# A selective-scan recurrence: some drives scaled on ScalarE in turned layout, other shared states, z projected at the start of the unit

## The chip, the cores and the metric

One core of one Trainium2 chip runs the whole kernel. The metric is device time in microseconds of one launch. The engines named below are TensorE (PE, its weight loads PEld), VectorE (DVE), ScalarE (ACT), GpSimd (POOL) and SyncE (SP), which here issues the DMA transfers of the recurrence. PSUM is 8 banks of 128 x 512 f32; four tiles of two banks each are all of it in this stage.

## The reference, cut to what matters

The input is (4, 64, 32, 32). A bidirectional Mamba layer with a group norm comes first, then attention, then a spectral filter with mixed experts. The change touches the first only. For each of 4 images, in both directions:

```python
xz = x @ W_in                               # 64 -> 256, halves xp and z
xc = silu(xprev * conv_w[:, 0] + xp * conv_w[:, 1] + conv_b)
dt_r, Bc, Cc = split(xc @ W_x)              # 8, 16, 16
dt = softplus(dt_r @ W_dt + b_dt)           # 128 channels
h = exp(dt * A[s]) * h + (dt * xc) * B[s]   # for each of 16 states s, over 1024 tokens
y = sum over s of h[s] * C[s] + D * xc
y = y * silu(z);  out = y @ W_out           # then group norm, silu, residual
```

## The kernel before, in words

A **unit** is one image in one direction: 8 units, u = 0 to 7, the image's forward one (i = 0) and then its backward one (i = 1). Tiles are [128 channels, 1024 tokens] f32. Unit 0 and 1 are written out, units 2 to 5 are a loop over images, units 6 and 7 are written out again, and unit 7 (the final one) also does the start of the attention of the first image. Everything runs in program order on each engine; semaphores tie the engines together.

Each unit runs 16 states. For a state, in the ordinary (own) form: ACT makes the decay exp(dt * a[s]) in one of three SBUF tiles (`decay_of`, L731); DVE multiplies dt*x (in PSUM, `ps_x`) by the row B[s], which a DMA has spread over 128 partitions (`b_wide`), into `ps_d` (`drive_step`, L871), and scans (`scan_step`, L876, the scan itself L888) into one of four `hidden` tiles; POOL multiplies this by the spread row C[s] into one of four `prod` tiles (L455); PE adds the product to `ps_y` with an identity matmul (`sum_states`, L547), three states late (`Y_LAG`).

Five states of a unit, 2, 3, 6, 9 and 15, are **shared**: POOL makes the drive, from an SBUF copy of dt*x (`share`, L441, the multiply L445), and ACT writes the decay to PSUM (`shared_decay_of`, L737): for 3, 6 and 9 (`WIDE_SHARED`) into `ps_w`, for 2 and 15 into `ps_d`. Unit 7 shares only state 6.

`ps_w` also carries the preparation of the next unit v = u + 1, between those decays: the projection of z (`gate_in`, L493, after state 15 of the unit before has been summed, at s == 2) and ACT's copy of it (`take_z`, L668), the projection of xp (`conv_in`, L498) and `silu_input` (L674), `low_rank` (L504) and `take_low`, and `dt_in` (L511), which may start when the scan of the last wide shared state, 9, has read its decay. `softplus_exp` and `softplus_ln` (L699 to L720) are six ACT operations in a row; PE sums their parts in `ps_w` (L518 to L539), ACT takes dt (L722), DVE makes dt*x (`dt_x`, L857) ahead of the scan of state 15, and ACT copies it to SBUF (`keep_dtx`, L726). In ACT's order the decay of state s + 2 stands at s, ahead of what else is done at s; so the decays of states 13 and 14 stand behind softplus, which is at s == 10.

After the scan of state 1 DVE gates the sum of the unit before (`gate_of`, L864, the multiply L869): it waits until PE has added all its 16 products. After it PE starts `ps_y` anew with D*xc (`skip_in`, L541, a diagonal matmul), and in forward units first does the output product (`out_product`, L555), which ACT must have taken (`norm_take`, L686) before `skip_in`.

SP issues the loads in its own order: for each state a B row, which waits until the drive that used its buffer is done (four buffers), and the C row of the state before, which waits for a product (L372 to L394).

## Time and profile before

| | us |
|---|---|
| median of 3 runs | 949.39 (944.57 to 951.92) |
| the profiled execution | 949.59 |
| its span | 947.8 |
| mean granted TensorE clock | 0.955 |
| units 0 to 7 with what leads to them | about 0 to 488 |

The page gives the busy time of each engine over the span; the windows give it by stretch. The timelines of the engines list instructions in order of time, runs of like ones merged, with the idle time before them and what ended it. A matmul with f32 operands of 512 columns appears as two records, so one `sum_states` is four. Throughout, T is the time from the start of the scan of state 15 of the unit before.

### The profile page before, as it was taken

Reading aid. Unit: us, or ns where it says so; the run is one execution under the profiler, and the core shown is the slowest. Engines: PE = TensorE matmul, PEld = TensorE weight load, DVE = VectorE, ACT = ScalarE, POOL = GpSimd, SP = SyncE. Lnnn points to the kernel's source line nnn. Section 1 sums busy time; section 2 is a strip of 40 time slices with the busy share of each in tenths; the row PEclk is TensorE's granted clock in tenths of the full one; section 3 lists DMA queues with packets and bytes.
Section 4 is the critical chain, followed back from the end, with each engine's and each line's share of the span. In section 5 each row is a group of like instructions: output and inputs, shape, how many; then the busy total and the mean of one; then the engine's idle time right before and its main releaser. Section 6 shows DMA issues by size and latency. Waiting matters only on the chain. (4 is left out here: it accounts for less than half of the span.)

```text
span 947.8 us, 10164 instructions
## 1 busy us (share of the span) xinstructions
PE 830.0 (88%) x2974; PEld 488.3 (52%) x2974; DVE 712.0 (75%) x767; ACT 508.8 (54%) x702; POOL 549.8 (58%) x373
## 2 busy tenths in 40 slices
PE   5579897979899898986587899989999999999996
PEld 1224332433334333332144554558888888888885
DVE  1999999999999999999965455646665665565664
ACT  3645666556566666643315446446555554555553
POOL 4678989999998998975736955312212221212210
PEclk9799999999999999987987999999999999999999
DMA  7969897888979898796509800001442443243342
GB/s 180 329 201 331 311 339 277 334 309 307 311 271 379 301 321 304 285 333 222 201 0 139 155 0 1 1 1 53 125 133 92 130 125 98 90 133 99 123 116 61
DMA packets 75348, 178.22 MB, mean 188 GB/s; under 512 B 24514, under 2 KB 25044, under 8 KB 75300
## 3 DMA queue, kind: packets, MB, share of 16 engines
q1 hardware_dynamic: 75316, 177.85, 57.9%
q8 instruction: 13, 0.21, 0.1%
q14 instruction: 19, 0.16, 0.1%
HBM read 175.57 MB, written 2.26 MB: 188 GB/s over the span
## 5 line engine op out<-in xcount | busy, mean ns | idle before, releaser
L455 POOL TENSOR_TENSOR prod<-hidden,c_wide 128x1024 f32<-128x1024 f32 x128 | 300.3, 2358 | 63.5 <-DVE hidden L888 58.1
L551 PE MATMUL ps_y<-prod,ident 128*128 128x512 f32 x512 | 242.8, 618 | 30.8 <-POOL prod L455 30.6
L888 DVE TENSOR_TENSOR_SCAN hidden<-decay,ps_d 128x1024 f32<-128x1024 f32 x92 | 209.9, 2282 | 8.3
L1919 PE MATMUL ps_conv<-hankel,u_high 128*128 128x512 f32 (+1 forms) x768 | 215.3, 361 | 0.0
L551 PEld LDWEIGHTS ps_y<-prod,ident 128*128 128x128 f32 x512 | 98.2, 197 | 171.3 <-issue 117.4
L1919 PEld LDWEIGHTS ps_conv<-hankel,u_high 128*128 128x128 f32 x768 | 138.6, 189 | 25.5 <-DVE u_t L1786 0.2
L1919 PE MATMUL ps_conv<-hankel,u_low 128*128 128x512 f32 (+1 forms) x384 | 138.1, 360 | 0.0
L2033 DVE TENSOR_TENSOR stack<-ps_conv,stack 64x512 fp32r<-64x512 f32 x128 | 88.3, 690 | 62.1 <-ACT stack L2000 59.6
L1751 POOL CAST block_mix<-even 128x256 fp32r (+1 forms) x32 | 12.7, 398 | 208.5 <-PE sums L1792 208.5
L2033 DVE TENSOR_TENSOR qk<-ps_conv,qk 64x512 fp32r<-64x512 f32 x128 | 88.3, 689 | 50.2 <-ACT qk L2000 47.5
L874 DVE TENSOR_TENSOR ps_d<-ps_x,b_wide 128x1024 f32<-128x1024 f32 x92 | 113.4, 1232 | 4.6
L2000 ACT ACTIVATE stack<-ps_conv 64x512 fp32r<-64x512 f32 x128 | 76.0, 594 | 74.3 <-PE ps_conv L1919 72.4
L2000 ACT ACTIVATE qk<-ps_conv 64x512 fp32r<-64x512 f32 x128 | 76.0, 593 | 63.2 <-PE ps_conv L1919 61.2
L445 POOL TENSOR_TENSOR drive<-dtx,b_wide 128x1024 f32<-128x1024 f32 x36 | 84.9, 2359 | 7.5 <-ACT dtx L729 7.1
L1919 PEld LDWEIGHTS ps_conv<-hankel,u_low 128*128 128x128 f32 x384 | 72.8, 190 | 13.8
L734 ACT ACTIVATE decay<-dt_b,a_neg_b 128x1024 f32<-128x1024 f32 x48 | 53.2, 1140 | 35.9 <-DVE hidden L888 35.6
L888 DVE TENSOR_TENSOR_SCAN hidden<-ps_w,drive 128x1024 f32<-128x1024 f32 x22 | 50.1, 2279 | 0.0
L734 ACT ACTIVATE decay<-dt_f,a_neg_f 128x1024 f32<-128x1024 f32 x44 | 48.2, 1137 | 2.0 <-DVE dt_f L852 0.9
L1472 DVE TENSOR_REDUCE max_parts<-sums 128x1 f32<-128x512 f32 (+1 forms) x48 | 27.5, 598 | 26.6 <-PE sums L1147 17.0
L1060 POOL TENSOR_TENSOR small<-small,minus_half 128x8 f32<-128x8 f32 x4 | 6.6, 1646 | 56.4 <-DVE small L1442 56.4
L1340 ACT ACTIVATE probs<-ps_t 128x512 f32<-128x512 f32 (+1 forms) x48 | 24.8, 521 | 22.8 <-PE ps_o L1192 22.4
L1792 PE MATMUL sums<-stack,block_mix 128*128 128x512 f32 (+1 forms) x160 | 32.5, 349 | 2.1 <-DVE stack L2033 2.1
(283 smaller groups left out, 1154.3 us busy)
## 6 DMA issues: line engine op xcount, KB each, us to landing
b_wide<-bc_rows SPq DMA_DIRECT2D x128, 512.0 KB, 5.6
c_wide<-bc_rows SPq DMA_DIRECT2D x128, 512.0 KB, 5.5
hankel<-filters SPq DMA_DIRECT2D x32, 1026.0 KB, 5.3
plus<-in_M_phi_plus SPq DMA_DIRECT2D x2, 1024.0 KB, 12.9
minus<-in_M_phi_minus SPq DMA_DIRECT2D x2, 1024.0 KB, 18.1
x_pair<-in_x SPq DMA_DIRECT2D x2, 768.0 KB, 8.3
bc_rows<-mixed_and_low SPq DMA_DIRECT2D x8, 128.0 KB, 4.9
out<-plus SPq DMA_DIRECT2D x4, 256.0 KB, 5.0
```

Of the source, the lines that this page charges most:

```text
L445: nc.gpsimd.tensor_tensor(drive[DRIVE_OF[s]][:, :], dtx[:, :], b_wide[s % BC_DEEP][:, :], ALU.mult).then_inc(share_ready, 1)
L455: nc.gpsimd.tensor_tensor(prod[k % PAIR][:, :], hidden[k % DEEP][:, :], c_wide[s % BC_DEEP][:, :], ALU.mult).then_inc(prod_ready, 1)
L551: mm = nc.tensor.matmul(out, ident[:, :], halves(prod[k % PAIR])[h], start=False, stop=(k % N == N - 1))
L734: nc.scalar.activation(decay[decay_slot(s, last)][:, :], dt[i][:, :], ACT.Exp, scale=a_neg[i][:, s:s + 1]).then_inc(decay_ready, 1)
L874: nc.vector.tensor_tensor(ps_d[:, :], ps_x[:, :], b_wide[s % BC_DEEP][:, :], ALU.mult).then_inc(drive_ready, 1)
L888: nc.vector.tensor_tensor_scan(hidden[k % DEEP][:, order], left[:, order], right[:, order], 0.0, ALU.mult, ALU.add).then_inc(hidden_ready, 1)
L1340: nc.scalar.activation(probs[n % 2][:, 0:hi - lo], ps_t[n % 2][:, 0:hi - lo], ACT.Exp).then_inc(probs_ready, 1)
L1472: nc.vector.tensor_reduce(max_parts[:, i, at // H:at // H + 1], ps_s[c % 2][:, 0:n], AX.X, ALU.max, negate=True).then_inc(part_ready, 1)
L1792: return nc.tensor.matmul(dst, w_block, data, start=first, stop=True, skip_group_check=True)
L1919: mm = nc.tensor.matmul(out, pairs[q][wp][:, 2 * delta + source, :], rows, start=(delta == 0 and term == 0), stop=(delta == 2 * half + 1 a ...
L2000: nc.scalar.activation(stacks[slot][0:C, source, b, :, half * 2 * HEAD:(half + 1) * 2 * HEAD], ps_conv[source][lanes(b), half, :, :], ACT. ...
L2033: nc.vector.tensor_tensor(low, ps_conv[source][lanes(b), half, :, :], high.bitcast(F32), ALU.subtract).then_inc(conv_low, 1)
```

## The change

- The shared states are 3, 7, 10, 15, of which 3, 7 and 10 are wide (in unit 7: state 6).
- States 2, 4, 8, 11 (in unit 7: 2, 7) are **turned**: PE transposes dt*x and the rows of B once per unit (`turn_dtx`, 8 + 8 transposes of 128 tokens, into `ps_w`), ACT copies them to SBUF (`take_turned`, three copies). With tokens on partitions, B[s] is a column, and ACT scales 8 tiles of 128 x 128 with it (`scale_drive`, 8 instructions); PE transposes the 8 back into `ps_d` (`turn_drive`), and DVE scans from there. DVE has no `drive_step` for these and SP no B row.
- `gate_in` stands at s == 0 and waits for the three copies; `take_z`, the decays and the new work have other places in ACT's order.
- `dt_in` stands at s == 11 and waits for the scan of state 10; the exponential's sum stands at s == 13 and the logarithm's at s == 14.
- D*xc is written to `ps_y` by ACT (`skip_in`, with a scale per channel) instead of by PE, and relu(dt) stays in `ps_w` instead of being added by PE. There is one `xc` tile instead of two.
- Three `b_wide` buffers instead of four, used in turn by the 12 states that still need a row.

```diff
-POOL_STATES = (2, 3, 6, 9, 15)
-WIDE_SHARED = POOL_STATES[1:4]
+POOL_STATES = (3, 7, 10, 15)
+TURNED_STATES = (2, 4, 8, 11)
+WIDE_SHARED = POOL_STATES[0:3]
+B_DEEP = 3
...
+        LAST_SHARE = (6,)
+        LAST_TURNED = (2, 7)
...
                 def spread_b(u, i, s):
-                    if u or s >= BC_DEEP:
-                        drive_done(*divmod(u * N + s - BC_DEEP, N))
-                    spread(b_wide[s % BC_DEEP], i * 2 * N + s, b_in[s % BC_DEEP])
+                    slot = b_slot(i, s, u // 2 == B - 1)
+                    if slot in held:
+                        drive_done(*held[slot])
+                    held[slot] = u, s
+                    spread(b_wide[slot], i * 2 * N + s, b_in[slot])
...
                 def gate_in(u, i, b):
-                    pe.wait_ge(dtx_ready, u)
+                    pe.wait_ge(dtx_t_ready, 3 * u)
                     project(i, b, w_gate[i], z_ready)
...
+                def turn_dtx(u):
+                    def turn(half):
+                        for t in range(half * SPANS, (half + 1) * SPANS):
+                            mm = nc.tensor.transpose(ps_w[:, t * 128:(t + 1) * 128], dtx[:, t * 128:(t + 1) * 128], ident[:, :])
+                        mm.then_inc(dtx_turned, 1)
+                    pe.wait_ge(dtx_kept, u + 1)
+                    turn(1)
+                    for t in range(TILES):
+                        mm = nc.tensor.transpose(ps_w[:, t * C:(t + 1) * C], dt_low[BC_ROW:, t * 128:(t + 1) * 128],
+                                                 ident[BC_ROW:, BC_ROW:])
+                    mm.then_inc(dtx_turned, 1)
+                    pe.wait_ge(dtx_t_ready, 3 * u + 2)
+                    turn(0)
+                def turn_drive(u, s, last=False):
+                    scanned(u, s - (2 if s - 1 in wide(last) else 1))
+                    for half in range(2):
+                        pe.wait_ge(drive_t_ready, 2 * turned_before(u, s, last) + half + 1)
+                        for t in range(half * SPANS, (half + 1) * SPANS):
+                            mm = nc.tensor.transpose(ps_d[:, t * 128:(t + 1) * 128], drive_t[turned_slot(s, last)][:, t, :], ident[:, :])
+                    mm.then_inc(drive_turned, 1)
...
                             if s == Y_LAG:
+                                turn_drive(u, s - 1, not ahead)
                                 if i == 0 and not first:
                                     out_product(b - 1)
+                                if s + 1 in turned(not ahead):
+                                    turn_drive(u, s + 1, not ahead)
+                                if i == 0 and not first:
                                     conv_in(v, j, bv)
-                                    pe.wait_ge(g.mixed_ready, b)
-                                skip_in(u, i)
-                            if s == 13 and ahead:
+                            if s == 14 and ahead:
                                 add_logarithm(v, j)
                             if not (first and k < Y_LAG):
-                                sum_states(n - Y_LAG, (k - Y_LAG) % (2 * N))
+                                sum_states(n - Y_LAG, (k - Y_LAG) % (2 * N), u if s == Y_LAG else None)
+                            if s > Y_LAG and s + 1 in turned(not ahead):
+                                turn_drive(u, s + 1, not ahead)
                             if ahead:
-                                if s == 2:
+                                if s == 0:
...
                                     gate_in(v, j, bv)
...
-                                if s == (7 if i == 1 or first else 5):
+                                if s == (8 if i == 1 or first else 7):
                                     scanned(u, WIDE_SHARED[1])
                                     low_rank(v, j)
-                                if s == 10:
+                                if s == 11:
                                     scanned(u, WIDE_SHARED[2])
                                     dt_in(v, j)
-                                if s == 11:
-                                    add_rectified(v)
-                                if s == 12:
+                                if s == 13:
                                     add_exponential(v)
+                                if s == N - 1:
+                                    turn_dtx(v)
...
+                def skip_in(u, i, taken=0):
+                    at_least(act, gated_ready, u)
+                    at_least(act, g.mixed_ready, taken)
+                    nc.scalar.activation(ps_y[:, :], xc[:, :], ACT.Copy, scale=cols[i][:, 1:2]).then_inc(skip_ready, 1)
+                def take_turned(u):
+                    def take(n, half):
+                        act.wait_ge(dtx_turned, 3 * u + n + 1)
+                        nc.scalar.activation(dtx_t[:, half * SPANS:(half + 1) * SPANS, :].rearrange("p t d -> p (t d)"),
+                                             ps_w[:, half * H:(half + 1) * H], ACT.Copy).then_inc(dtx_t_ready, 1)
+                    at_least(act, drive_turned, TURNED * u)
+                    take(0, 1)
...
+                    take(2, 0)
+                def scale_drive(u, s, last=False):
+                    act.wait_ge(dtx_t_ready, 3 * u + 3)
+                    at_least(act, drive_turned, turned_before(u, s, last) - 1)
+                    for t in range(TILES):
+                        part = nc.scalar.activation(drive_t[turned_slot(s, last)][:, t, :], dtx_t[:, t, :], ACT.Copy, scale=b_t[:, t, s:s + 1])
+                        if t % SPANS == SPANS - 1:
+                            part.then_inc(drive_t_ready, 1)
...
+                            if s == 0:
+                                take_z(v, j, first=first and i == 0)
+                                shared_decay_of(u, i, WIDE_SHARED[0], z_taken, v)
+                                decay_of(u, i, 2)
+                            if s == 1:
+                                scale_drive(u, 4)
+                                decay_of(u, i, 4)
                             if s == 2:
...
+                                decay_of(u, i, 5)
...
+                                if first or i == 1:
+                                    skip_in(u, i)
                                 silu_gate(v, j)
                                 if not first:
                                     if i == 0:
                                         norm_take(b - 1)
+                                        skip_in(u, i, taken=b)
                                     else:
                                         norm_silu(nc, act, g, b - 1)
                                 silu_input(v, j)
...
                             if s == 4:
+                                decay_of(u, i, 6)
                                 shared_decay_of(u, i, WIDE_SHARED[1], xc_ready, v + 1)
+                            if s == 5:
+                                scale_drive(u, 8)
+                            if s == 6:
+                                decay_of(u, i, 8)
+                                decay_of(u, i, 9)
...
+                                scale_drive(u, 11)
                             if s == 7:
                                 take_low(v, j)
                                 shared_decay_of(u, i, WIDE_SHARED[2], dt_low_ready, v + 1)
+                            if s in (9, 10, 11, 12):
+                                decay_of(u, i, s + AHEAD)
...
                             if s == N - 1:
...
                                 keep_dtx(v)
                                 decay_of(v, j, 1, last and i == 0)
+                                take_turned(v)
+                                if TURNED_STATES[0] in turned(last and i == 0):
+                                    scale_drive(v, TURNED_STATES[0], last and i == 0)
```

## Rows read from the trace of the kernel before

**Rows 1.** Windows: busy time by stretch, granted clock, DMA share
```profile
core 0: us, PE busy (x) PEld busy (x) DVE busy (x) ACT busy (x) POOL busy (x), PEclk, DMA share, GB/s
...
230.00:300.00 70.00, 64.74 (x143) 26.13 (x143) 67.67 (x41) 44.34 (x44) 64.39 (x29) 0.98 0.90 322
```

**Rows 2.** Line L729 (dtx copied), all eight, and the second alone
```profile
L729 ACT ACTIVATE dtx<-ps_x x8: 1024/1024/1030, 28.0 to 409.7; 128x1024 f32<-128x1024 f32 x8
...
L729 ACT ACTIVATE dtx<-ps_x x1: 1030/1030/1030, 86.1 to 86.1; 128x1024 f32<-128x1024 f32 x1
```

**Rows 3.** Timeline of DVE: start, us, instruction, in unit 4
```profile
246.53 1.21 DVE L862 TENSOR_TENSOR ps_x<-ps_w,xc_f 128x1024 f32<-128x1024 f32 x1
247.80 2.29 DVE L888 TENSOR_TENSOR_SCAN hidden<-ps_d,drive 128x1024 f32<-128x1024 f32 x1
...
257.44 1.20 DVE L869 TENSOR_TENSOR gated_b<-ps_y,gate_b 128x1024 f32<-128x1024 f32 x1
...
271.56 2.28 DVE L888 TENSOR_TENSOR_SCAN hidden<-ps_w,drive 128x1024 f32<-128x1024 f32 x1
273.76 2.26 DVE L888 TENSOR_TENSOR_SCAN hidden<-decay,ps_d 128x1024 f32<-128x1024 f32 x1
276.15 1.23 DVE L874 TENSOR_TENSOR ps_d<-ps_x,b_wide 128x1024 f32<-128x1024 f32 x1
...
279.81 1.23 DVE L874 TENSOR_TENSOR ps_d<-ps_x,b_wide 128x1024 f32<-128x1024 f32 x1
280.95 2.28 DVE L888 TENSOR_TENSOR_SCAN hidden<-ps_w,drive 128x1024 f32<-128x1024 f32 x1
```

**Rows 4.** Timeline of PE: sums, the wait for the gate, dt_in
```profile
242.52 8.75 PE L551 MATMUL ps_y<-prod,ident 128*128 128x512 f32 x20
...
258.69 1.97 PE L560 MATMUL ps_y<-gated_f,packed_inner_f 128*64 128x512 f32 x2 [2.41 <-DVE gated_b L869]
...
284.44 1.98 PE L514 MATMUL ps_w<-mixed_and_low,w_dt_b 9*128 9x512 f32 x4
```

**Rows 5.** Timeline of POOL in unit 4
```profile
270.20 6.98 POOL L455 TENSOR_TENSOR prod<-hidden,c_wide 128x1024 f32<-128x1024 f32 x3 [0.90 <-PE ps_y L551]
277.13 2.37 POOL L445 TENSOR_TENSOR drive<-dtx,b_wide 128x1024 f32<-128x1024 f32 x1
279.45 9.29 POOL L455 TENSOR_TENSOR prod<-hidden,c_wide 128x1024 f32<-128x1024 f32 x4
```

**Rows 6.** Timeline of PE: eight transposes of a later stage
```profile
643.46 1.06 PE L1772 MATMUL ps_conv<-ident,u_all 128*128 128x128 f32 x8 [1.14 <-PEq L1044]
```

**Rows 7.** Timeline of ACT in a later stage: eight scaled tiles
```profile
577.69 2.01 ACT L1302 ACTIVATE u_all<-cen,small 128x64 f32<-128x64 f32 x8
```

**Rows 8.** Timeline of ACT, end of unit 3 and in unit 4
```profile
234.69 1.06 ACT L713 ACTIVATE late<-soft 128x1024 f32<-128x1024 f32 x1
...
237.69 2.17 ACT L734 ACTIVATE decay<-dt_b,a_neg_b 128x1024 f32<-128x1024 f32 x2
...
247.85 1.02 ACT L729 ACTIVATE dtx<-ps_x 128x1024 f32<-128x1024 f32 x1
...
286.46 1.03 ACT L704 ACTIVATE soft<-ps_w 128x1024 f32<-128x1024 f32 x1 [4.99 <-PE ps_w L514]
...
289.37 1.06 ACT L713 ACTIVATE late<-soft 128x1024 f32<-128x1024 f32 x1
```

**Rows 9.** Windows of 6 us: the granted clock is the third number from the end
```profile
96.00:102.00 6.00, 4.92 (x8) 2.01 (x8) 5.84 (x4) 5.51 (x5) 6.00 (x3) 0.72 0.76 273
...
366.00:372.00 6.00, 5.22 (x8) 1.37 (x8) 5.84 (x4) 5.21 (x5) 6.00 (x3) 0.72 0.75 263
...
420.00:426.00 6.00, 5.28 (x7) 2.24 (x8) 5.70 (x5) 2.44 (x4) 3.68 (x2) 0.51 0.82 291
```

**Rows 10.** Timelines of DVE and PE in the first unit
```profile
36.63 2.29 DVE L888 TENSOR_TENSOR_SCAN hidden<-ps_d,drive 128x1024 f32<-128x1024 f32 x1 [1.19 <-ACT ps_d L740]
...
26.82 3.50 PE L486 MATMUL ps_w<-x_pair,packed_in_b 128*128 128x512 f32 x4 [4.15 <-DVE ps_x L854]
```

More of the change, by code:

```diff
@@ L297, in mamba_stage, with wide, turned, decayed_before @@
         AHEAD = 2
-        LAST_SHARE = POOL_STATES[2:3]
+        LAST_SHARE = (6,)
+        LAST_TURNED = (2, 7)
         def shared(last):
             return LAST_SHARE if last else POOL_STATES
+        def wide(last):
+            return LAST_SHARE if last else WIDE_SHARED
+        def turned(last):
+            return LAST_TURNED if last else TURNED_STATES
         def driven_before(u, s, last=False):
+            return (N - SHARE - TURNED) * u + s - sum(p < s for p in shared(last) + turned(last))
+        def decayed_before(u, s, last=False):
             return (N - SHARE) * u + s - sum(p < s for p in shared(last))
@@ L307, in shared_before, with turned_before, spread_order, b_slot @@
             return SHARE * u + sum(p < s for p in shared(last))
+        def turned_before(u, s, last=False):
+            return TURNED * u + sum(p < s for p in turned(last))
+        def spread_order(last):
+            return [(i, s) for i in range(2) for s in range(N) if s not in turned(last and i == 1)]
+        UNIT_LOADS = N - TURNED
+        def b_slot(i, s, last):
+            return spread_order(last).index((i, s)) % B_DEEP
+        def b_loads(b, i, s, last):
+            return 16 * (2 * UNIT_LOADS // B_DEEP * b + spread_order(last).index((i, s)) // B_DEEP + 1)
+        def turned_slot(s, last):
+            return turned(last).index(s) % 2
         def own_states(last):
@@ L383, in unit @@
                     for s in range(N):
-                        spread_b(u, i, s)
+                        if s not in turned(u == 2 * B - 1):
+                            spread_b(u, i, s)
                         if u or s:
@@ L475, in _ @@
                 pool.wait_ge(x_in, X_LOADS)
-                share(0, POOL_STATES[0])
                 batch(0, first=True)
@@ L553, in sum_states @@
+                def sum_states(n, k, seeded=None):
+                    pe.wait_ge(prod_ready, n + 1)
+                    if seeded is not None:
+                        pe.wait_ge(skip_ready, seeded + 1)
+                    for h, out in enumerate(halves(ps_y)):
+                        mm = nc.tensor.matmul(out, ident[:, :], halves(prod[k % PAIR])[h], start=False, stop=True,
+                                              skip_group_check=True)
                     mm.then_inc(prod_summed, 1)
@@ L735, in decay_of, with shared_decay_of @@
                                          scale=a_neg[i][:, s:s + 1]).then_inc(decay_ready, 1)
-                def shared_decay_of(u, i, s, taken, count):
+                def shared_decay_of(u, i, s, taken, count, final=False):
                     act.wait_ge(taken, count)
-                    nc.scalar.activation((ps_w if s in WIDE_SHARED else ps_d)[:, :], dt[i][:, :], ACT.Exp,
+                    nc.scalar.activation((ps_w if s in wide(final) else ps_d)[:, :], dt[i][:, :], ACT.Exp,
                                          scale=a_neg[i][:, s:s + 1]).then_inc(share_decay, 1)
@@ L882, in scan_step @@
                         dve.wait_ge(share_ready, shared_before(u, s, final) + 1)
-                        left, right = (ps_w if s in WIDE_SHARED else ps_d), drive[DRIVE_OF[s]]
+                        left, right = (ps_w if s in wide(final) else ps_d), drive[DRIVE_OF[s]]
                     else:
-                        dve.wait_ge(decay_ready, driven_before(u, s, final) + 1)
-                        dve.wait_ge(drive_ready, driven_before(u, s, final) + 1)
+                        dve.wait_ge(decay_ready, decayed_before(u, s, final) + 1)
+                        if s in turned(final):
+                            dve.wait_ge(drive_turned, turned_before(u, s, final) + 1)
+                        else:
+                            dve.wait_ge(drive_ready, driven_before(u, s, final) + 1)
                         left, right = decay[decay_slot(s, final)], ps_d
@@ L930, in batch @@
                                 dve.wait_ge(dtx_kept, 1)
-                            if s in shared(final) and s in WIDE_SHARED:
-                                drive_step(u, s + 1, final)
-                            elif s not in shared(final) and not (s - 1 in shared(final) and s - 1 in WIDE_SHARED):
-                                drive_step(u, s, final)
+                            if s not in shared(final) + turned(final):
+                                drive_step(b, i, s, last)
                             scan_step(u, i, s, final)
```

114 lines of the change are left out of this document (55 added, 59 removed).

## The prediction

> **What bounds the kernel now.** I read the windows by stretch first, to see which engine is full in the recurrence; then the times of the dt*x copies, which mark the units; then the timelines of DVE, ACT, PE and POOL through one unit; then the clock by windows of 6 us. In [rows 1] DVE is busy 67.67 of 70 us, POOL 64.39, PE 64.74 at a granted clock of 0.98 (2.4 GHz), ACT 44.34: DVE sets the pace, with POOL and PE close behind. The copies of dt*x lie at 28.0, 86.1 and 409.7, eight in all [rows 2]: the first unit takes 58.1 us, and the next six (409.7 - 86.1)/6 = 53.93 us each.
>
> DVE's unit can be rebuilt from [rows 3]. An own state, drive and dependent scan, recurs after 279.81 - 276.15 = 3.66 us. A scan that needs no drive costs 273.76 - 271.56 = 2.20. dt_x costs 247.80 - 246.53 = 1.27 and the gate the same. Eleven own and five shared states give 11 x 3.66 + 5 x 2.20 + 2.5 = 53.8, and the norm's few steps 0.3 on average: the 53.93 is DVE with no gap. PE's sum costs 8.75/5, less the modelled tail, 1.72 us; POOL's multiply (9.29 - 2.37)/3 = 2.31 [rows 4, 5].
>
> **The change, part by part.**
>
> *DVE.* Three drives a unit go (11 to 8), each 3.66 - 2.20 = 1.46. The pure work becomes 8 x 3.66 + 8 x 2.20 + 2.5 + 0.3 = 49.7 us, 4.2 less. A scan that reads what PE turned costs the same as one that reads a drive in PSUM, I assume; no row differs.
>
> *PE.* Eight transposes of this shape and type took 1.06 us [rows 6]. A unit has 48 (8 of dt*x, 8 of B, 32 of drives): 6.4 us. It loses the D*xc product and the relu part, 2 x 1.72 = 3.4. It was about 26 blocks of 1.72 = 44.7 in 53.9, and becomes 47.7: no bound by itself. The Trainium skill ("TensorE: Matmul & The Clock Gate", Part 4: PE-mode transpose) gives about 275 ns for a 128 x 128 transpose inside a kernel: 48 of them would be an estimated 13.2 us in place of 6.4. A record here does last some 0.27 us, but they overlap and eight end after 1.06, so the row decides.
>
> *POOL.* 20 multiplies instead of 21, 46.2 us, and one norm or residual step; not the bound in total.
>
> *ACT.* Per turned state 8 scaled tiles. The nearest row is eight of 128 x 64 in 2.01 us [rows 7]; at 128 columns I take 2.35. The lower end is 2.01, the upper one eight with the extra half of the columns unhidden, about 2.8. Four states are 9.4 us, the three copies 1.6 (halves of the 1.02 copy [rows 8]), skip_in 1.1: from 44.34/70 x 53.9 = 34 us to 46. Below DVE's 49.7, but in strict order, so places matter.
>
> *DMA.* 28 row loads a unit instead of 32, at a share of 0.90 [rows 1]. Following the buffers, the row of state 15 waits for the drive of 12 and lands about a microsecond before POOL wants it. I cost it at 0; if it is late, POOL's share of 15 is late by as much.
>
> **Where the gain goes: the start of the unit.** T = 0 is the start of scan 15. dt*x is in SBUF at 1.05 [rows 8]. ACT makes decay 1 until 2.15; PE turns half of dt*x and then B until 2.7; ACT copies both until 3.1; PE turns the other half until 3.75, ACT copies it by 4.4 and scales state 2 by 6.8. All of that round trip lies ahead of PE's sum of state 13, because turn_dtx stands before it in PE's order. So: sum 13 to 5.5, the z projection to 7.3, sum 14 to 9.0, sum 15 to 10.8. The gate waits for sum 15. DVE reaches it at 257.44 - 247.80 = 9.64 today [rows 3]. **Stall 1.2 us**, and behind the gate stand all later scans. The transposes of state 2 (10.8 to 11.8) hide behind the gate.
>
> **The softplus chain.** dt_in writes `ps_w`, so it waits for the last wide shared scan, which was 9 and is now 10. From the start of dt_in to ACT's first step is 286.46 - 284.44 = 2.02 [rows 4, 8]; from there to the fourth operation 289.37 - 286.46 = 2.91; from the fourth to the end of the decay behind the chain, 237.69 + 1.13 - 234.69 = 4.13. Together 9.1 us until decay 13 is there. Between the end of scan 10 and the start of scan 13 DVE has 2.20 + 3.66 + 1.34 = 7.2 of work. **Stall at least 1.9 us in every unit**; before, there was one more drive-and-scan between, 11 us, and the chain just fitted. Moreover dt_in stands behind the sum of state 8, which waits for POOL's product 8, which now comes behind the share of state 10. Following POOL at 2.31 a step: in backward units product 8 is done at 35.5, after a PE backlog dt_in starts at 37.5, decay 13 is there at 46.6, and the next unit's T = 0 is 7.2 later (scan 13, state 14, dt_x): **53.8**. In forward units ACT does the gate's silu and norm_take ahead of skip_in, so the sum of state 0 ends at 21.4, POOL's product 4 starts there (today after a like wait, at 270.20, T + 22.4 [rows 5]), share 10 ends at 35.3, product 8 at 37.6, dt_in starts at 39.4, decay 13 at 48.5: **55.6**. Six units: 3 x 53.8 + 3 x 55.6 = 328.2 against 323.6: **+4.6**.
>
> **First and last unit.** In the first, the round trip and scale 2 take ACT and PE to 36.5, and the z projection is at half clock (3.50 [rows 10] instead of the 1.98 of such four records [rows 4], so I count the transposes double): scan 2 waits for decay 2 until 40.2 instead of 36.63 [rows 10], +3.6; three drives fewer behind it, -4.4; softplus +2.9: **+2.1**. The last unit has no z projection, so sum 15 is in time; it drops two drives, **-2.9**; ACT waits for DVE there and takes the new work in its gaps.
>
> **The clock.** In five of these six units PE's clock fell right after its 2.41 us wait for the gate [rows 4]: the first and last are at 0.72 over 6 us [rows 9], so 6 x 0.28 = 1.7 us lost, half of that stretch at 1.2 GHz. In the last unit, transposes and a 3 us wait were followed by 0.51 [rows 9]. In the new order the thin stretch (wait for dt*x, transposes, round trip) stands right ahead of the four blocks that lead to the gate, so a dip there is on the path: 1.7 us a unit, and nothing absorbs it, as ACT's order shifts with it. I take it in three units of six, **+5.1**; bounds 0 and 10.
>
> Sum: 4.6 + 2.1 - 2.9 + 5.1 = +8.9, on the profiled execution's 949.6: 958.5. That execution and the median of the runs (949.4) agree, so the forecast is 958.5.
>
> **The rivals.**
>
> *A. Only the unavoidable stalls.* If product 8 is never late and no dip is on the path, a unit is 49.7 + 1.2 + 1.9 = 52.8: 6 x -1.1 = -6.8, first unit +1.1, last -2.9: -8.6, 941. For it: POOL is caught up at the end of each unit today, and the gate and chain numbers are tight. Against: the backlog is visible today in PE's run of five sums up to dt_in.
>
> *B. The gain arrives.* If the round trip and the chain are covered, 6 x -4.2, first -0.8, last -2.9: -29, 921. It needs dt_in's chain to be 2 us shorter than the rows; nothing in them says so. The place to see it is decay 13.
>
> *C. Slower by one mechanism, the clock.* A dip in every unit ahead of the gate, twice as long (all four blocks at 3.4 instead of 1.7): 6 x 6.9 = 41 over the 3.8 without dips: 994; with a normal dip in every unit, 10 + 3.8: 963. It decides above 0.9 us a unit. The final unit's row speaks for it; no row shows a whole unit start. The Trainium skill ("TensorE: Matmul & The Clock Gate", Part 4: PE-mode transpose) says that the full clock does not engage for transposes; by that it would be the 994.
>
> *D. ACT's order.* If eight scaled tiles cost 2.8, decays 7 and 10 and the drives of 8 and 11 each come 0.5 to 1.5 late: 1.5 a unit more, 968.
>
> **How the numbers follow.** Forecast (53.8 and 55.6, some dips; 953 to 963): 0.42. A: 0.20. B and what lies between it and A: 0.12. C in its long form and D: 0.26. The range takes A in and D, and leaves out B and C's long form: 940 to 971; the forecast's own is 953 to 963. About 1% (9.5 us) is what a measurement of this kernel can tell from no change. Faster (below 939.9) is B and a part of A: 0.19. Slower (above 958.9) is half of the forecast, C and D: 0.44. The same: 0.37.
>
> **What would show it.** Right: the copies of dt*x 54 to 56 us apart; DVE idle 1 to 3 us before L869's gate, ended by PE's sum, and 2 to 3.6 us before the scan of state 13, ended by ACT's decay; POOL and PE idle more. Transposes of eight in about 1.1 us, eight scaled tiles in 2.0 to 2.8. Wrong: copies closer than 52 us (B); DVE waiting for `ps_d` transposes or for shared decays (D); a mean clock in the recurrence well under 0.9 (C); waits on the B rows. The forecast fails most easily if PE reaches sum 15 before DVE reaches the gate.

## The result and the profile after

The changed kernel takes 980.2 us (977.5 to 983.4), the kernel before 948.7 beside it: 1.033 times as long, with a 95% interval of 1.030 to 1.036. That is slower, as the likeliest sign of the forecast had it, and 9 us outside the range of 940 to 971. The span of the profiled execution went from 947.8 to 975.7 us.

The copies of dt*x mark the units, as in [rows 2]. The line of all eight, and those that begin units 1 to 3 (each from its own stretch), from the changed kernel:

```profile
L792 ACT ACTIVATE dtx<-ps_x x8: 1002/1024/1025, 25.9 to 440.7; 128x1024 f32<-128x1024 f32 x8
...
L792 ACT ACTIVATE dtx<-ps_x x1: 1025/1025/1025, 86.5 to 86.5; 128x1024 f32<-128x1024 f32 x1
...
L792 ACT ACTIVATE dtx<-ps_x x1: 1024/1024/1024, 144.3 to 144.3; 128x1024 f32<-128x1024 f32 x1
L792 ACT ACTIVATE dtx<-ps_x x1: 1024/1024/1024, 204.9 to 204.9; 128x1024 f32<-128x1024 f32 x1
```

The first unit takes 60.6 us (58.1 before). The six after it take (440.7 - 86.5)/6 = 59.0 each, against 53.9: 30.6 us in all. From there to the end of the span is 535.0 us against 538.1. The first copy comes 2.1 us earlier. So +2.5 - 2.1 + 30.6 - 3.1 = +27.9, the whole difference, and it lies in units 1 to 6. (The 2.1 us belong to the start of the program and are not the change's: in the kernels below this copy comes at 25.5 to 28.3.)

The windows over these six units, of the changed kernel and then of the one before (columns as in [rows 1]):

```profile
86.50:440.70 354.20, 314.48 (x864) 145.20 (x864) 292.37 (x171) 271.40 (x412) 285.60 (x126) 0.92 0.72 252
```
```profile
86.10:409.70 323.60, 289.16 (x627) 116.20 (x626) 313.10 (x189) 200.75 (x194) 298.46 (x132) 0.97 0.87 313
```

DVE has 21 us less work and yet the stretch is 31 us longer; the clock is 0.92 instead of 0.97. In the kernel before, DVE's waits in this stretch are too short to be listed. These are its waits now (line waited for, us in total, times, longest):

```profile
DVE hidden L1001 <- ACT decay L820: 29.1, 9, 6.2
DVE gated_f L978 <- PE ps_y L605: 9.4, 3, 3.7
DVE gated_b L978 <- PE ps_y L605: 6.9, 3, 3.6
DVE hidden L1001 <- POOL drive L484: 5.8, 5, 1.9
DVE hidden L1001 <- PE ps_d L596: 2.9, 6, 0.6
DVE hidden L1001 <- issue: 0.5, 1, 0.5
```

They sum to 54.6 us. The removed work was worth 6 x 4.2 = 25 by the rebuilding of the prediction; that leaves a loss of about 30, as the copies have it. What is open here is why the waits are that long, and whether each is a place of its own or one delay seen several times.

In the timeline, a forward unit (4, T = 262.6): DVE and then PE of the changed kernel.

```profile
272.96 1.23 DVE L978 TENSOR_TENSOR gated_b<-ps_y,gate_b 128x1024 f32<-128x1024 f32 x1 [0.78 <-PE ps_y L605]
...
299.56 2.29 DVE L1001 TENSOR_TENSOR_SCAN hidden<-ps_w,drive 128x1024 f32<-128x1024 f32 x1 [1.95 <-POOL drive L484]
...
312.90 2.29 DVE L1001 TENSOR_TENSOR_SCAN hidden<-decay,ps_d 128x1024 f32<-128x1024 f32 x1 [3.45 <-ACT decay L820]
```
```profile
263.51 0.66 PE L578 MATMUL ps_w<-ident,dtx 128*128 128x128 f32 x4 [0.89 <-ACT dtx L792]
264.09 0.71 PE L584 MATMUL ps_w<-ident,mixed_and_low 64*128 64x64 f32 x8
265.20 0.66 PE L578 MATMUL ps_w<-ident,dtx 128*128 128x128 f32 x4 [0.39 <-ACT b_t L804]
265.70 1.98 PE L605 MATMUL ps_y<-prod,ident 128*128 128x512 f32 x4
267.52 1.88 PE L524 MATMUL ps_w<-x_pair,packed_in_b 128*128 x4
269.24 3.60 PE L605 MATMUL ps_y<-prod,ident 128*128 128x512 f32 x8
...
303.69 1.98 PE L552 MATMUL ps_w<-mixed_and_low,w_dt_b 9*128 9x512 f32 x4
```

This is the path that the prediction wrote down: round trip, sum 13, z, sums 14 and 15, gate; then dt_in, which starts at T + 41.1 where 39.4 was forecast. Unit 3 has the same order with the clock down:

```profile
205.95 1.12 PE L578 MATMUL ps_w<-ident,dtx 128*128 128x128 f32 x4 [3.11 <-ACT dtx L792]
207.00 1.11 PE L584 MATMUL ps_w<-ident,mixed_and_low 64*128 64x64 f32 x8
208.48 1.12 PE L578 MATMUL ps_w<-ident,dtx 128*128 128x128 f32 x4 [0.37 <-ACT b_t L804]
209.39 3.34 PE L605 MATMUL ps_y<-prod,ident 128*128 128x512 f32 x4
```

Sum 13 takes 3.3 us instead of 2.0; it came after an idle time of 3.11 us and the transposes. That is so in five of the six units (3.2 to 3.6 us for it, idle 2.2 to 3.1 before the first transposes); only unit 4, with 0.89 us of idle, keeps 2.4 GHz on the way to its gate.

There is a second place of this kind, between the gate and dt_in. In backward units the transposes of state 4 wait for the scan of state 2, which is behind the gate. The rows of PE in units 1, 3 and 5:

```profile
103.93 3.75 PE L605 MATMUL ps_y<-prod,ident 128*128 128x512 f32 x4 [0.81 <-ACT ps_y L741]
107.47 3.10 PE L524 MATMUL ps_w<-x_pair,w_conv_f 128*128 128x512 f32 x4
...
222.24 1.70 PE L596 MATMUL ps_d<-ident,drive_t 128*128 128x128 f32 x8 [3.48 <-DVE hidden L1001]
223.73 3.00 PE L605 MATMUL ps_y<-prod,ident 128*128 128x512 f32 x4
...
337.65 1.09 PE L596 MATMUL ps_d<-ident,drive_t 128*128 128x128 f32 x8 [3.49 <-DVE hidden L1001]
338.70 3.60 PE L605 MATMUL ps_y<-prod,ident 128*128 128x512 f32 x4
```

From there PE has no idle time until dt_in (127.95, 245.88, 361.43), so what these blocks take too long, 3.0, 1.7 and 1.7 us, delays dt_in. In forward units it is the sum of state 8, right ahead of dt_in, after a wait of 2.2 us for POOL's product: 3.68 us in unit 2, and in unit 6 2.97 with 3.78 for dt_in itself; unit 4 has neither.

### The profile page after: what moved, and what is told of

It reads as the page before. It is cut to its first block and busy times, and to the rows that moved or that the text cites. A ratio compares the mean times of both kernels' runs of the same rounds, so it can differ in the third digit from the quotient of the medians.

```text
span 975.7 us, 11050 instructions
## 1 busy us (share of the span) xinstructions
PE 856.8 (88%) x3282; PEld 524.1 (54%) x3282; DVE 681.3 (70%) x742; ACT 598.0 (61%) x974; POOL 534.5 (55%) x366
## 5 line engine op out<-in xcount | busy, mean ns | idle before, releaser
L605 PE MATMUL ps_y<-prod,ident 128*128 128x512 f32 x512 | 259.4, 653 | 29.7 <-POOL prod L494 16.2
L1001 DVE TENSOR_TENSOR_SCAN hidden<-decay,ps_d 128x1024 f32<-128x1024 f32 x99 | 226.0, 2283 | 47.8 <-ACT decay L820 39.7
L605 PEld LDWEIGHTS ps_y<-prod,ident 128*128 128x128 f32 x512 | 102.4, 208 | 161.7 <-issue 127.3
L2028 PEld LDWEIGHTS ps_conv<-hankel,u_high 128*128 128x128 f32 x768 | 138.6, 189 | 25.5 <-DVE u_t L1895 0.2
L1860 POOL CAST block_mix<-even 128x256 fp32r (+1 forms) x32 | 12.7, 398 | 208.5 <-PE sums L1901 208.5
L984 DVE TENSOR_TENSOR ps_d<-ps_x,b_wide 128x1024 f32<-128x1024 f32 x69 | 85.0, 1232 | 4.0
L820 ACT ACTIVATE decay<-dt_b,a_neg_b 128x1024 f32<-128x1024 f32 x51 | 56.9, 1140 | 27.3 <-DVE hidden L1001 26.7
L813 ACT ACTIVATE drive_t<-dtx_t,b_t 128x128 f32<-128x128 f32 x240 | 73.1, 386 | 0.6
L484 POOL TENSOR_TENSOR drive<-dtx,b_wide 128x1024 f32<-128x1024 f32 x29 | 68.5, 2361 | 8.6 <-DMA b_wide<-bc_rows 7.4
L820 ACT ACTIVATE decay<-dt_f,a_neg_f 128x1024 f32<-128x1024 f32 x48 | 53.0, 1138 | 1.3 <-DVE dt_f L961 0.9
L596 PE MATMUL ps_d<-ident,drive_t 128*128 128x128 f32 x240 | 34.0, 288 | 19.0 <-DVE hidden L1001 19.0
L596 PEld LDWEIGHTS ps_d<-ident,drive_t 128*128 128x128 f32 x240 | 29.3, 148 | 35.0 <-issue 19.9
```

What stands on the lines that cost most here:

```text
L484: nc.gpsimd.tensor_tensor(drive[DRIVE_OF[s]][:, :], dtx[:, :], b_wide[slot][:, :], ALU.mult).then_inc(share_ready, 1)
L596: mm = nc.tensor.transpose(ps_d[:, t * 128:(t + 1) * 128], drive_t[turned_slot(s, last)][:, t, :], ident[:, :])
L605: mm = nc.tensor.matmul(out, ident[:, :], halves(prod[k % PAIR])[h], start=False, stop=True, skip_group_check=True)
L813: part = nc.scalar.activation(drive_t[turned_slot(s, last)][:, t, :], dtx_t[:, t, :], ACT.Copy, scale=b_t[:, t, s:s + 1])
L820: nc.scalar.activation(decay[decay_slot(s, last)][:, :], dt[i][:, :], ACT.Exp, scale=a_neg[i][:, s:s + 1]).then_inc(decay_ready, 1)
L984: nc.vector.tensor_tensor(ps_d[:, :], ps_x[:, :], b_wide[slot][:, :], ALU.mult).then_inc(drive_ready, 1)
```

## The experiments

Each kernel was timed beside the kernel before. The ratio to it, with its 95% interval, is the figure to compare across groups of runs. Where no other engine is named, the waits below are DVE's over units 1 to 6 of the profiled execution.

| kernel | us | ratio |
|---|---|---|
| changed | 980.2 | 1.033 (1.030 to 1.036) |
| e1: decay 13 first | 955.3 | 1.010 (1.006 to 1.013) |
| e2: z later | 974.4 | 1.028 (1.024 to 1.032) |
| e3: e1 and e2 | 951.2 | 1.004 (1.001 to 1.007) |
| e4: store later | 972.8 | 1.026 (1.022 to 1.031) |
| e12: e1 and e4 | 943.8 | 0.997 (0.995 to 1.000) |
| e5: e1, e2 and e4 | 936.7 | 0.988 (0.986 to 0.990) |
| e6: e5, sums earlier | 938.0 | 0.990 (0.987 to 0.993) |
| e7: filler | 967.8 | 1.021 (1.018 to 1.024) |
| e8: z twice | 989.4 | 1.043 (1.040 to 1.046) |
| e9: e5 and filler | 942.1 | 0.994 (0.992 to 0.996) |
| e10: e5, decays swapped | 940.9 | 0.991 (0.988 to 0.994) |
| e11: e5, filler, swap | 947.6 | 0.999 (0.997 to 1.001) |

### e1: the decay of state 13 ahead of the softplus chain

```diff
-                            if s in (9, 10, 11, 12):
+                            if s in (9, 10, 12):
                                 decay_of(u, i, s + AHEAD)
                             if s == 10:
+                                decay_of(u, i, 13)
                                 softplus_exp(v, j, squared=b if i == 0 else 0)
```

> The changed kernel (980.2 us) with one move: on ACT the decay of state 13 is issued ahead of the softplus chain instead of behind it. Its buffer is free once scan 9 is done, and ACT sits idle for 7 us there before dt_in is ready, so the move itself costs nothing. Theory 1 (the softplus chain behind dt_in is where most of the time went: 29.1 us of DVE idle before scans whose decay is late, nine waits in units 1 to 6): the waits of 3 to 6 us before scan 13 vanish, the copies of dt*x come 55 to 56 us apart instead of 59.0, and the time falls by 20 to 26 us, to 954 to 960. Rival 1 (POOL and PE are behind at that point anyway): DVE meets the next wait at once, for POOL's drive of state 15 or for PE's sum of the softplus parts ahead of dt_x, and under 8 us is gained: above 972.

Measured: 955.3, 24.9 us less. DVE's waits for decays fall from 29.1 to 5.5 us, those for POOL's drives stay, and waits of 6.1 for dt ahead of dt*x and 5.4 for the decay of state 15 appear (two stretches of the list):

```profile
DVE hidden L1002 <- POOL drive L484: 6.1, 5, 2.0
DVE hidden L1002 <- ACT decay L820: 5.5, 4, 2.8
DVE hidden L1002 <- ACT ps_d L826: 5.4, 5, 1.1
DVE ps_x L972 <- ACT dt_f L787: 3.4, 2, 2.0
```

Theory 1 holds: most of the loss was one instruction's place. Its buffer was free, ACT was idle, and the wait was order alone. The waits before the gates fell too, from 16.3 to 5.2, and with them PE's idle time ahead of its first transposes, over all eight units from 23.0 to 12.7 us. The reading: without the stall before scan 13 PE is not through with its sums long before dt*x comes, it idles less there, and its clock holds more often.

### e2 and e8: the z projection later, and twice

```diff
-                                if s == 0:
+                                if s == 2:
...
                                     gate_in(v, j, bv)
...
                             if s == 0:
-                                take_z(v, j, first=first and i == 0)
-                                shared_decay_of(u, i, WIDE_SHARED[0], z_taken, v)
                                 decay_of(u, i, 2)
                             if s == 1:
                                 scale_drive(u, 4)
                                 decay_of(u, i, 4)
+                                take_z(v, j, first=first and i == 0)
+                                shared_decay_of(u, i, WIDE_SHARED[0], z_taken, v)
```

> The changed kernel with the z projection put back behind the sum of state 15 on PE (s == 2), and ACT's copy of z and the decay of state 3 behind the scaling of state 4. Theory 2 (the gate waits because dt*x's round trip and the z projection stand ahead of sums 14 and 15; 16.3 us of DVE idle before six gates): the projection's 1.72 us leave the path, and at half clock 3.4; DVE's idle before the gates falls from 16.3 to 4 to 7 us, the time by about 10 us, to 970. Rival 2 (only the clock's dips make the gate late, wherever z stands): the idle before the gates falls by 3 us at most, and the time stays within 4 us of 980.

Measured: 974.4, 5.7 us less, for the 10 expected. The waits before the gates fall from 16.3 to 6.5 us, as expected, but 5.5 of the 9.8 us come back: waits for turned drives go from 2.9 to 8.4, since z now stands ahead of the transposes of state 2.

e8 leaves z where the change put it and does it twice:

```diff
                     pe.wait_ge(dtx_t_ready, 3 * u)
+                    for h, out in enumerate(halves(ps_w)):
+                        nc.tensor.matmul(out, w_gate[i], x_flat[:, bass.ds(b * (L + 1) + i + h * H, H)], start=True, stop=True)
                     project(i, b, w_gate[i], z_ready)
```

> The changed kernel with the z projection done twice in the same place (the second overwrites the first): 1.72 us more on PE between the round trip and sums 14 and 15. Theory 2 (this is the path to the gate, and nothing behind it absorbs a delay): each of six units gets 1.7 us longer or more where the clock is down: 11 to 16 us, 991 to 996. Rival 2 (the gate has slack, or the later stall at scan 13 absorbs it): under 4 us, 980 to 984.

Measured: 989.4, 9.2 more, and by the ratios 1.0% or 9.7 us: over units 1 to 6, 1.6 us each for 1.72 us of work. DVE's waits before the gates are 28.9 instead of 16.3. It lies a little under the 991 expected and well above the rival's 984: this stretch of PE is on the path at nearly its full price.

### e4 and e12: SP's store of the norm's sums behind the B row

```diff
-                            if s == 9:
+                            if s == 10:
                                 store_sums(sp, g, u // 2 - 1)
```

> The changed kernel with one move on SP: the store of the group norm's sums stands at s == 10, behind the B row of state 10, instead of ahead of it at s == 9. In unit 4 SP stood there for 5.2 us waiting for ACT's squares, which the new order puts behind the scaling of state 8, and the B row of state 10 was issued late; POOL waited 1.4 us for it and DVE 1.95 us for POOL's drive. Theory 3: forward units (2, 4, 6) lose these waits, about 1.5 us each, and with dt_in that much earlier the time falls by 3 to 5 us, to 976. Rival 3 (three buffers instead of four are the cause): the row stays late, no gain.

Measured: 972.8, 7.3 less. POOL in unit 4, the changed kernel and then e4:

```profile
288.62 7.02 POOL L494 TENSOR_TENSOR prod<-hidden,c_wide 128x1024 f32<-128x1024 f32 x3
297.06 2.37 POOL L484 TENSOR_TENSOR drive<-dtx,b_wide 128x1024 f32<-128x1024 f32 x1 [1.41 <-DMA b_wide<-bc_rows]
```
```profile
286.89 6.99 POOL L494 TENSOR_TENSOR prod<-hidden,c_wide 128x1024 f32<-128x1024 f32 x3
293.85 2.35 POOL L484 TENSOR_TENSOR drive<-dtx,b_wide 128x1024 f32<-128x1024 f32 x1
```

The wait is gone with three buffers still in use, so the rival falls for this row. The gain, above the 3 to 5 us expected, is larger than such waits: PE's idle time ahead of the sum of state 8 falls from 2.2 to 2.4 us to 1.0 in all three forward units, and the half clock behind it is gone in units 2 and 6 (sum 1.98 for 3.68 and 2.97, dt_in 1.98 for 3.78). Units 2, 4 and 6 become 2.9, 1.5 and 4.0 us shorter; unit 4, which had no half clock there, gains the wait alone. POOL still waits 6.0 us in four waits for other B rows, about as much as before (6.2 in five), yet DVE's waits for POOL's drives fall from 5.8 to 1.9. Whether a fourth buffer would end the rest was not tried.

> The changed kernel with the decay of state 13 moved and the store moved, the z projection left where the change put it. Known: the decay move alone 955.3, with z 951.2, all three 936.7; so the store's move was worth 14.6 us behind the other two and 7.3 us alone. Theory: the late B row holds POOL, PE then idles and comes to dt_in at half clock (in the kernel with two moves PE's clock was 0.60 and 0.54 over 12 us of unit 4, behind a wait for POOL), and that is what the store's move saves, wherever z stands: 955.3 less 10 to 15, 940 to 945. Rival: it needs the z move as well; less than 8 us gained, above 947.

Measured: 943.8, as the theory had it. In e3, where the B row is still late, PE waited 2.13 us for POOL in unit 4 and then ran dt_in at half clock:

```profile
282.17 2.76 PE L605 MATMUL ps_y<-prod,ident 128*128 128x512 f32 x4 [2.13 <-POOL prod L494]
284.86 3.78 PE L552 MATMUL ps_w<-mixed_and_low,w_dt_b 9*128 9x512 f32 x4
288.57 6.12 PE L605 MATMUL ps_y<-prod,ident 128*128 128x512 f32 x8
```

That unit took 60.5 us, where unit 3 ahead of it took 54.6. In the profile of e12 the granted clock there stays at 1.0. There PE waits 0.98 us, and dt_in takes 1.98. So the late row cost more than its wait: it idled PE at the spot where the next product is dt_in.

### e3, e5, e6: the moves together

> Both moves, of the decay of state 13 and of the z projection. If the two stalls are independent, the gains add: 30 to 36 us less than 980, 944 to 950, about the kernel before. If one only uncovers the other or the backlog of POOL and PE, the gain is little more than the larger one alone: 954 or more.

Measured: 951.2, 28.9 less than the changed kernel, near the 30.6 of the two gains added; not quite the forecast 944 to 950. Its ten runs fall in two groups, 944.6 to 948.9 us at a clock of 0.951 to 0.957 and 953.6 to 955.7 at 0.939 to 0.944, and the profile is of the first; so how well the gains add is known to some 5 us only.

> The changed kernel with three moves: the decay of state 13 ahead of the softplus chain, the z projection behind the sum of state 15, the store of the norm's sums behind the B row of state 10. Before this run: the first alone took 24.9 us off the 980.2, the second 5.7, the third 7.3, the first two together 28.9. If the late B row still holds POOL's drive of state 10 (7.8 us of waits for B rows in the kernel with two moves), three forward units gain 1 to 1.5 us each: 945 to 948, within 0.5% of the kernel before. Rival (with the softplus stall gone the late row is hidden): no gain over the two moves, 951.

Measured: 936.7, below the forecast 945. The three gains alone add up to 38 us, together they are 43. Most of the surplus can be seen beside e3: units 2, 4 and 6 take 53.3 us each for 54.7, 60.5 and 54.7, so in unit 4 the late row cost 7.2 us with the half clock behind it and 1.4 in the others without. Against the kernel before it is 1.2% faster (0.986 to 0.990). Its windows over the same six units:

```profile
82.50:399.00 316.50, 291.85 (x865) 135.39 (x864) 292.59 (x171) 269.34 (x412) 285.33 (x126) 0.99 0.82 281
```

52.8 us a unit at a clock of 0.99, with the same work on every engine as in the changed kernel (DVE 292.6, ACT 269.3, POOL 285.3). It is the same arithmetic in another order.

e6 puts PE's parts of softplus back to where they were before the change:

```diff
-                            if s == 14 and ahead:
+                            if s == 13 and ahead:
                                 add_logarithm(v, j)
...
-                                if s == 13:
+                                if s == 12:
                                     add_exponential(v)
```

> The three moves, and PE adds the exponential's part at s == 12 and the logarithm's at s == 13, where they were before, one product sum earlier. In the kernel with two moves DVE waits 5.3 us in four waits for dt ahead of dt*x. Theory: PE stood behind a product of POOL there; the waits go down by 2 to 4 us, to 942 to 946. Rival: PE is then held by the chain while products pile up, and POOL waits for PE; no gain.

Measured: 938.0, no gain. DVE's waits for dt fall from 3.1 to 2.2 us, and those for turned drives rise from 3.1 to 6.2.

### e7 and e9: a filler against the clock

```diff
                 def turn_dtx(u):
...
+                    if not isinstance(u, int) or u:
+                        for t in range(TILES):
+                            nc.tensor.matmul(ps_y[:, t * 128:(t + 1) * 128], none[:, :], ident[:, :], start=False, stop=True,
+                                             skip_group_check=True)
                     pe.wait_ge(dtx_kept, u + 1)
```

> The changed kernel, with 8 matmuls of 128 columns on a zero weight tile added to ps_y at the end of each unit, ahead of PE's wait for dt*x (about 1.7 us of work in a gap of 0.9 to 3.1 us): nothing of the result changes. Theory 4 (half clock after this gap lengthens the path to the gate; the granted clock at the starts of units 2, 3, 5, 6 is 0.6 to 0.8 over 6 us): fewer dips there, DVE's idle before the gates falls from 16.3 to 8 to 12 us, the time to 972 to 976. Rival (the dip comes from the transposes and the round trip behind the gap, or it only moves): the gates' idle and the time stay as they are, 978 to 984, as fillers also take PE's time.

Measured: 967.8, 12.4 less than the changed kernel, with more work on PE. The waits before the gates fall from 16.3 to 8.7 us, and the clock from 84 us to the end of unit 6 is 0.96 instead of 0.92:

```profile
84.00:430.00 346.00, 313.01 (x974) 153.03 (x972) 294.96 (x174) 273.27 (x412) 287.44 (x126) 0.96 0.73 260
```

The 7.6 us of gate waits explain 7.6 of the 12.4; the long wait of unit 6 (6.24 us, with dt_in at half clock) is not there either. The time fell below the 972 to 976 expected. The clock was a cause of its own, and keeping PE at work removed part of it, but not all: in unit 2 the idle time is down to 1.31 us and sum 13 still takes 3.50, while in unit 6 the sum of state 8 keeps 1.98 after 2.66 us of idle. So the length of the idle time just before does not settle by itself which level comes.

> The three moves (936.7 us) and the filler of 8 small matmuls ahead of PE's wait for dt*x. With the filler alone the time went from 980.2 to 967.8, as the clock then stayed up on the way to the gate. Theory: in the kernel with three moves the granted clock in units 1 to 6 is already 0.99 (84 to 400 us) and DVE does not wait for PE before its gates, so the filler has nothing to save: 934 to 939. Rival: dips still cost several us in the timed runs, and the filler gives 3 us or more: under 934.

Measured: 942.1, 0.6% slower than e5 by the ratios. There was nothing left to save, as the theory said, but the cost was not nil: the filler ends at 87.0 in unit 1, after dt*x is ready, and waits for turned drives rise from 3.1 to 6.6.

### e10 and e11: the decay of state 15 ahead of that of state 0

```diff
-                            if s == 14:
-                                decay_of(v, j, 0, last and i == 0)
...
                                 keep_dtx(v)
-                                decay_of(v, j, 1, last and i == 0)
+                                decay_of(v, j, 0, last and i == 0)
                                 take_turned(v)
+                                decay_of(v, j, 1, last and i == 0)
```

> The three moves, and on ACT the decay of state 0 of the next unit behind the decay of state 15 and the copy of dt*x, the decay of state 1 behind the three copies of turned data. With three moves DVE waits five times 1.1 us for ACT's decay of state 15, which stands behind that of state 0. Theory: these 5.4 us go, and with them 4 to 6 us of the time: 931 to 933. Rival: the round trip of the turned data starts a decay later or PE's sum 15 becomes late, and the gain is under 2 us.

Measured: 940.9, and by the ratios no gain but a loss of 0.3%, which the two intervals do not settle. The 5.4 us before the scan of state 15 went, and 4.2 us more of waits for other decays, 2.7 for decays in `ps_w` and 1.6 for POOL's drives came.

> The three moves, the filler and the swap of the decays together. If the swap gains and the filler has nothing to save, the same as with the swap alone: 931 to 934. If shorter units bring the path to the gate back and dips with it, the filler helps here by 2 to 4 us over the swap alone.

Measured: 947.6, 1.1% above e5. Neither case that was forecast: the losses of e9 (0.6%) and e10 (0.3%) about add up. DVE waits before the gates again (4.3 us, none listed in e5) and 9.1 us for turned drives (3.1 in e5); that both moves delay the start of the unit is the likely reading.

## Why the prediction was right and wrong

**The sign and the mechanisms were right.** The gain of 25 us in DVE's work was eaten by the two stalls that the prediction named. They were found where it put them, by the releasers that it named: gates ended by PE's sums, scan 13 ended by ACT's decay. e1, e2 and e8 confirm both as causes. The two short terms came out close as well: the first unit +2.5 us for +2.1, the last part -3.1 for -2.9. In the first unit the parts hold too: the scan of state 2 came 12.4 us behind that of state 0 (12.15 by the forecast's 40.2), and the stall before scan 13 was 3.1 for 2.9. Rival B, that the gain arrives, is excluded for the kernel as changed.

**The costs of the new instructions were right.** Eight transposes took 1.04 us (1.06 taken), eight scaled tiles 2.45 (2.35 taken):

```profile
272.67 1.04 PE L596 MATMUL ps_d<-ident,drive_t 128*128 128x128 f32 x8
```
```profile
266.60 2.45 ACT L813 ACTIVATE drive_t<-dtx_t,b_t 128x128 f32<-128x128 f32 x8
```

So rival D's cause is out. Six times the 1.04 is 6.2 us for the 48 transposes of a unit.

The prediction's estimate of 13.2 us for them goes by the 275 ns of the Trainium skill ("TensorE: Matmul & The Clock Gate", Part 4: PE-mode transpose), which are given there for bf16, while the tiles here are f32. The trace agrees with this as the duration of one record (median 273 ns), but not as a cost: the records overlap.

**What failed was the size of the six units, 9.7 us forecast (4.6 of stalls and 5.1 of dips) and 30.6 found.** The step that failed is the hand schedule from the start of a unit to dt_in. It put dt_in at T + 37.5 in backward and at T + 39.4 in forward units. It started at T + 41.0 to 41.4 in the backward ones (units 1, 3, 5) and at 44.2, 41.1 and 44.7 in the forward ones. The chain behind it was right: 9.2 us (unit 4: 303.69 to 312.9) for the forecast 9.1, and 11.0 in unit 6, where dt_in itself ran at half clock. So the six units took 57.7, 60.6, 57.6, 57.6, 57.7 and 62.9 us, where 53.8 and 55.6 in turn were forecast. Three things made dt_in late; the shares are estimates from the rows.

*The clock ahead of the gate.* Three dips of 1.7 us were taken. Five of six units had them, after 2.2 to 3.1 us of idle time ahead of dt*x. The waits before the gates were 16.3 us, where 1.2 in each unit and the three dips make 12.3: 4 us too few.

*The clock between the gate and dt_in.* This term the prediction put at nothing: it wrote this stretch down at full clock, though its own [rows 9] have dips of the kernel before just behind the gate, where no wait of DVE came of them. (It says that they came right after the wait for the gate; in unit 3 it was after a wait of 2.21 us for the scan of state 3.) The blocks shown above took too long by 3.0, 1.7, 1.7, 0, 1.7 and 2.8 us in the six units, 11 us in all, the largest share. For the forward units e4 shows it, as the dips went with the late row. For the backward ones it is read from the trace, since PE had no idle time from there to dt_in; no experiment took these dips alone away.

*SP's queue.* The prediction costed the B rows at 0 by following buffers only, and named waits on them as a sign of being wrong. It did not follow SP's order past the store of the norm's sums, which waits for ACT's squares, which the change put behind more of ACT's work. In unit 4 SP stood there 5.2 us with the row of state 10 behind it. The late row made PE's wait ahead of dt_in longer by 1.2 to 1.5 us in each forward unit, some 4 us, besides the dips. e4 shows 7.3 us for both and, in the kernel where decay 13 is early, e12 shows 11.5. The row of state 15, which was to land a microsecond early, was 1.8 us late in unit 1; no scan waited for its drive.

That is 19 of the 21 us. DVE's waits tell the same from the other end. Before scan 13 DVE waited 3.2, 5.1, 3.2, 3.5, 3.2 and 6.2 us, 24.4 in all, about the 23 that the forecast's own units imply: dt_in was late, but DVE had been held on its way too. The rest are the 16.3 before the gates and 13.9 that were put at nothing: 4.7 for the decay of state 6 in the three backward units (ACT stood ahead of it waiting for the projection of xp, which is behind the gate and in one case itself at half clock), 5.8 for POOL's drives, 2.9 for turned drives and 0.5.

The prediction had both stalls and the clock as separate terms, and left out that one feeds the other: scan 13's wait leaves PE idle ahead of dt*x, PE is then slow on the way to the gate, the late gate leaves it idle and slow once more, and dt_in comes late, which makes the next wait of scan 13. e1 supports this loop: with the wait of scan 13 gone, PE's idle time ahead of dt*x and the waits before the gates fell as well. The rival of half clock over all four blocks was too strong: of the blocks behind sum 13, z took 1.88 us, full clock, in three of the five units and 2.3 and 2.5 in the other two, and sums 14 and 15 were at full clock in all. The Trainium skill ("TensorE: Matmul & The Clock Gate", Part 4: PE-mode transpose) has the full clock not engage for transposes; the trace does not agree: in unit 4 all 16 of the round trip and the sums behind them ran at 2.4 GHz.

**A blind spot.** The prediction said that DVE would wait for decay 13 and called the stall unavoidable in rival A. It was unavoidable only in the order as written; the decay needed nothing of the chain. The same holds for the whole change: with three moves in the order it is 1.2% faster than before.

**What stays open.** The loss of e10 was not resolved further. The B rows that are still late with three buffers were not tested. Why PE's clock falls after some idle times and not after others of the same length is not shown. The loop through the clock is read from the traces and from what e1 did to the later waits; no kernel broke it at one place alone.

## What to carry to other kernels

Where a stretch was full on one engine and two others followed closely, a hand schedule gave the sign and the places of the stalls, but they fed each other, and its sum was a third of what was found. A clock dip that costs nothing in the kernel before is worth looking for in the rows: it costs once the path runs through it. After moving work in a queue, go through every instruction left behind it and ask whether it needs what now stands ahead of it: here one decay, one store and one projection were worth 43 us in 980. And follow the queue of SP as closely as those of the engines, through the instructions that wait for something else than a buffer.

## What was not expected of the hardware

In the changed kernel PE idled 2.2 to 3.1 us ahead of the small transposes of the round trip in five units, and the four records of 512 columns behind these took 3.2 to 3.6 us instead of 1.98; in the unit with 0.89 us of idle they did not. e7 shows that the idle time alone does not decide (3.50 us after 1.31, 1.98 after 2.66). Work of no use, 8 products of 128 columns adding zeros (1.95 us), made the changed kernel 12 us faster, and the one with three moves, where the gap was 0.8 us, 0.6% slower. Over the six units the granted clock was 0.92 of the full one in the changed kernel and 0.99 in the one with three moves, from the same instructions.
